# Unread bf16 products on TensorE in five of a quad's eight items of the maximum phase

## What is computed

```python
def _L1_gnn_ref(z, P, W1, b1, W2, b2, Wu, bu):
    m1z = z @ W1.T + b1
    m2z = z @ W2.T + b2
    pair = relu(m1z[:, :, None, :] + m2z[:, None, :, :])
    mask = (swapaxes(P, 1, 2) != 0)[..., None]
    m = max(where(mask, pair, -inf), axis=2)
    return relu(concatenate((z, m), axis=-1) @ Wu.T + bu)
...
h = maximum(layernorm(x), 0)
x = x + _L1_gnn_ref(h, adj, ...)
```

## Times and profile before

| | us |
|---|---|
| median of 3 timed runs | 2086.39 |
| range of them | 2083.98 to 2087.57 |
| the profiled execution | 2077.1 |
| its span, first to last instruction | 2075.3 |
| of it quad 0 of the maximum phase | 26.9 |
| quads 1 to 14 | 414.1 |
| quad 15 | 30.9 |

### The profile page before, as it was taken

The page is one execution under the profiler, slowest core; times in us unless marked ns, Lnnn a source line. Parts: engine busy times, 40 slices in busy tenths (PEclk is TensorE's granted clock), DMA queues, the critical chain, the costliest instruction groups (busy, mean ns, idle before and its releaser), DMA issues. The chain is left out here.

```text
span 2075.3 us, 43855 instructions
## 1 busy us (share of the span) xinstructions
PE 1737.3 (84%) x13771; PEld 1096.7 (53%) x13771; DVE 1727.0 (83%) x2689; ACT 1390.1 (67%) x3229; POOL 597.2 (29%) x449
## 2 busy tenths in 40 slices
PE   2966777777776899897799999999999678988886
PEld 1855556555663666665465555555555234444445
DVE  5878888888875777785799999999999577888887
ACT  0533333333334999895588888888888687888884
POOL 1530000000002544443344444444444211111110
PEclk9989998999887999997999999999999899999999
DMA  6000000000000000000055555555555699999993
GB/s 183 1 13 1 1 0 0 0 0 0 0 1 4 7 6 4 6 6 21 32 224 223 222 222 223 220 223 220 223 220 223 256 371 350 391 376 369 375 342 88
DMA packets 123567, 292.98 MB, mean 141 GB/s; under 512 B 21376, under 2 KB 57608, under 8 KB 123288
## 3 DMA queue, kind: packets, MB, share of 16 engines
q1 hardware_dynamic: 106360, 283.37, 35.9%
q10 hardware_dynamic: 16896, 8.39, 1.4%
q0 software_dynamic: 256, 0.56, 0.1%
HBM read 150.45 MB, written 141.82 MB: 141 GB/s over the span
## 5 line engine op out<-in xcount | busy, mean ns | idle before, releaser
L1316 POOL TENSOR_TENSOR pair_ring<-hd 128x2048 f32 (+1 forms) x64 | 269.5, 4211 | 310.1 <-DVE pair_ring L1341 310.1
L1401 ACT ACTIVATE v_hid<-v_psW 128x1024 f32<-128x1024 f32 x256 | 263.2, 1028 | 84.9 <-PE v_psW L1439 84.9
L771 DVE TENSOR_REDUCE m_part<-m_psS 128x128 f32<-128x2048 f32 (+1 forms) x128 | 258.9, 2023 | 66.1 <-PE m_psS L638 66.1
L1337 DVE TENSOR_TENSOR pair_ring<-v_psX,hd 128x2048 f32<-128x2048 f32 x128 | 292.3, 2289 | 17.1 <-PE v_psW L1439 17.1
L1439 PE MATMUL v_psW<-pair_ring,p_w1T 128*64 128x512 f32 x1024 | 288.5, 596 | 0.0
L1404 ACT ACTIVATE v_junk<-v_psW 128x1024 bf16<-128x1024 f32 x256 | 263.0, 1027 | 0.0
L638 PE MATMUL m_psS<-m_onehot,m_tableT 32*128 32x128 f32 x3584 | 151.8, 307 | 127.7 <-DVE m_part L771 123.4
L1439 PE MATMUL v_psW<-pair_ring,l_w1T 128*64 128x512 f32 (+1 forms) x1024 | 252.5, 587 | 0.0
L1430 PE MATMUL v_psW<-p_ends,v_weights 128*64 128x512 bf16 x1536 | 235.2, 381 | 3.1 <-DMA v_fold<-in_c_fold_dram 3.1
L638 PEld LDWEIGHTS m_psS<-m_onehot,m_tableT 32*128 32x128 f32 x3584 | 128.6, 207 | 147.3 <-issue 78.2
L708 ACT ACTIVATE m_tableT<-m_psTT 128x512 f32<-128x512 f32 (+1 forms) x128 | 69.3, 541 | 202.4 <-PE m_psTT L620 202.1
(11 more groups left out here) (260 smaller groups left out, 3354.9 us busy)
## 6 DMA issues: line engine op xcount, KB each, us to landing
pair_hidden<-v_hid SPq DMA_DIRECT2D x256, 512.0 KB, 2.6
pair_ring<-pair_hidden SPq DMA_DIRECT2D x128, 1024.0 KB, 7.7
adj_ring<-in_adj_dram ACTq DMA_DIRECT2D x16, 256.0 KB, 5.5
x_all<-in_x_dram ACTq DMA_DIRECT2D x16, 256.0 KB, 5.5
out_dram<-x_all SPq DMA_DIRECT2D x16, 256.0 KB, 2.3
pair_scores<-s_rot SPq DMA_DIRECT2D x64, 32.0 KB, 4.6
s_fwd<-pair_scores SPq DMA_DIRECT2D x64, 32.0 KB, 3.9
s_wide<-pair_scores SPq DMA_DIRECT2D x64, 32.0 KB, 5.0
```

The source lines that it names most:

```text
L771: nc.vector.tensor_reduce(part[:, i % 2, r, :], psS[:, :, 0:w].rearrange("z q (c i) -> z i q c", i=N), AX.XY, ALU.max).then_inc(reduced, 1)
L1316: nc.gpsimd.tensor_tensor(D[:, home(u, SLABS - 1), :].rearrange("c (h d i) -> c h d i", h=2, i=N), one, far, ALU.subtract).then_inc(psub_d ...
L1337: nc.vector.tensor_tensor(slab(s), own, windows(hd, n, s)[1], ALU.max).then_inc(max_done, 1)
L1401: nc.scalar.activation(hid[:, s, :], psW[:, buf, :], ACT.Identity, accum_out=hsum[:, bass.ds(m, 1)]).then_inc(evacuated, 1)
```

## The change

`busy` is a new function on TensorE. It waits until the copy of psF that was issued last for the next quad is done (the one of `second` in item 2, the one of `first` in the others), and then runs two bf16 products of 512 columns, the identity with the first 512 columns of the mask, both into psF. Nobody reads them. It is called at the end of items 2, 4, 5, 6 and 7 of every quad but the last.

```diff
@@ -653,6 +653,13 @@
                         last = nc.tensor.matmul(psU[:, b(i)], mT[:, p, b(i)], k.wuT[:, 1, :], start=False, stop=i == G - 1)
                     last.then_inc(u_mm, 1)
 
+                def busy(g, at):
+
+
+                    pe.wait_ge(m2_copied if at == 2 else m1_copied, done(g))
+                    for _ in range(2):
+                        nc.tensor.matmul(psF[:, :], k.identb[:, :], k.mask1[:, 0:QC], start=True, stop=True)
+
                 def quad(g, p, prev, next):
                     for at in range(ITEMS):
                         select(g, *divmod(at, NG))
@@ -670,6 +677,8 @@
                             prepare(g, *divmod(at + 2, NG))
                         elif next:
                             prepare(g + 1, *divmod(at + 2 - ITEMS, NG))
+                        if at in (2, 4, 5, 6, 7) and next:
+                            busy(g + 1, at)
                 turn(0, 0)
                 second(0, 0)
                 first(0, 0)
```

## The result

| | before | changed |
|---|---|---|
| median | 2083.93 us (6 runs) | 2058.93 us (6 runs) |
| range | 2071.26 to 2087.57 | 2046.81 to 2065.35 |
| the profiled execution | 2077.1 | 2046.81 |
| ratio, 95% interval | | 0.9884 (0.9852 to 0.9917) |

Two further comparisons of the same two kernels, on two different chips, gave 0.9875 (0.9829 to 0.9920) and 0.9897 (0.9854 to 0.9940). The change makes the kernel faster by 1.0 to 1.25%, 21 to 26 us by the three ratios; their intervals reach from 0.6 to 1.7%.

A forecast was written before the change was run, and what follows sets the result against it. Bound: rounds between TensorE and VectorE through one buffer psS, partly at half clock. 12.4 + 7.2 us returned, less 6.0 and 2.1 for item 5's pairs, save 11.5 us: from a median of 2086.39 to 2075 us, range 2064 to 2088.

The forecast's parts named there:

- The round of one buffer, and what is paid in it: Maximum phase, single buffer psS: TensorE work inside a reduction's time is free; whatever makes the selection longer or later is paid.
- The price of a pair: Two added products take 0.43 us at full clock or 0.85 at half; in item 5 about 0.4 us, 6.0 us over 15 quads.
- The new waits: Waits for m2_copied in item 2 and m1_copied in the others: taken as zero, at most 0.2 us in item 2.
- The second place of falls (items 6, 7, 0): Clock falls beginning at the end of item 6 or in item 7 vanish, returning 9.0 + 1.6 + 1.8 = 12.4 us.
- The first place (item 5): Falls beginning in item 5 after item 4's pause: half of 14.4 us returned, 7.2 us; 4 to 7 of 14 quads still fall.
- The sum: Maximum phase: 12.4 + 7.2 - 6.0 - 2.1 = 11.5 us saved.
- Together 26.8 us [...] This is the most that the change can return: Half-clock loss of items 5, 7, 6 and 0 over quads 1 to 14, taken as the upper bound on the saving there.
- quad 15 gets no added products: Last quad of the maximum phase: its next is false, so no pairs, and it was expected to stay as before.
- the first (all falls vanish): Quads 1 to 14: every fall vanishes, item 5 pays its pair; 20.8 us saved, 2065.6 us; chance 0.15.
- The second (the first place untouched, the second one gone): Item 5 falls as before, falls around items 6 and 7 vanish; 2.5 us saved, 2084 us; chance 0.18.
- The third (the clock isn't moved): Added products don't move the clock, or only move falls elsewhere; item 5 pays, 9.9 us slower, 2096 us; chance 0.12.
- The fourth (half of the second place returned): About half of the 12.4 us around items 6 and 7 returned, none in item 5; about no change, 2086 us; chance 0.09.

## Why the prediction was wrong

By its own steps:

- **The round of one buffer, and what is paid in it:** right. Pairs in the pauses of items 2, 4, 6 and 7 cost nothing at full clock: item 4 took 3.57 us with and 3.56 without, item 7 3.22 and 3.22.
- **The price of a pair:** right. Item 5 at full clock went from 3.48 to 3.90 us, 0.42 against the 0.4 taken. With a fall it took 5.52 to 5.57, within the 5.1 to 5.9 forecast.
- **The new waits:** free, as taken. Items 2 and 4 kept their length.
- **The second place of falls (items 6, 7, 0):** right. 12.4 us were forecast, and the first pair of profiles has 54.1 - 44.8 = 9.3 in item 7, 49.6 - 48.2 = 1.4 in item 6 and 59.1 - 56.7 = 2.4 in item 0, together 13.1 us.
- **The first place (item 5):** right in number, 6 of 14 slowed where 4 to 7 were forecast. With the price of its own pair the item lost 1.4 us, where the sum had a loss of some 0.5 in quads 1 to 14 (7.2 returned, 5.6 and 2.1 lost). The comparison on which the forecast rested, that a pause of 1.35 us or less had not been followed by a fall, did not hold: all six follow item 4's pause of 1.34 us.
- **The sum:** 11.5 us were forecast for the maximum phase, and quads 0 to 14 of the first two profiles differ by 11.25. So close a match is luck in part: the second place gave 0.7 us more, the first 0.9 less.

Against the base of this comparison, 2083.93 us, the saving was 25.0 us and not 11.4. That is 13.6 of the 16.1 us by which the time was missed; the other 2.5 are the base itself, 2086.39 in the forecast. The steps that failed are two terms of the bound on the saving, both read off one execution.

- **"Together 26.8 us [...] This is the most that the change can return":** this term was read from one execution, as if it were a property of the program. Over four profiles quads 0 to 14 took 441 to 455 us at a full-clock length near 414, so the half clock takes 27 to 41 us of them, 34 on average. The first profile showed the lower end. The changed kernel has been the same in all its profiles, so the missed part, some 7 us, is all saving. Even the rival in which all falls vanish had a saving of only 20.8 us by this bound, less than was measured.
- **"quad 15 gets no added products", hence no saving:** it has no pairs, but its length is not fixed: 26.5 to 29.0 us in the profiles of before, 24.5 to 26.3 in those of the changed kernel, 28.4 and 25.7 on average. These 2.7 us were not in the sum. They rest on few profiles, and no fall in the quads ahead is no cure: with the pauses filled quad 15 took 29.0 us again.

The terms 11.25, 6.7 and 2.7 make the 20.7 us of the traces. The range of 2064 to 2088 allowed for the cases of the change, and nothing for the base or for the bound; single runs of before alone cover 42 us.

Of the rivals, the first (all falls vanish) took place only where more of the pauses was filled. The second (the first place untouched, the second one gone) is nearest to the kernel with pairs in items 6 and 7 alone; it missed that the first place does not stay untouched. The third (the clock isn't moved) is what one-row products do, and what the full ones don't. The fourth (half of the second place returned) did not occur. The rule of the Trainium skill that the third names (TensorE: Matmul & The Clock Gate, "Why this matters for your kernels"), a fall after an idle pause longer than any in quads 0 to 14, doesn't describe these falls: they went away when pauses of 1.2 to 1.8 us were filled, and one-row products, with TensorE busier than before, didn't stop them. That transposes might not count was tried by no run.

What stays open: the intervals of the comparisons, 0.983 to 0.994, hold both the 20.7 us of the traces and the 25 us of the medians, so whether some 4 us more are saved elsewhere isn't settled. Why a given execution of before takes the shorter or the longer pattern isn't settled either.

## What to carry to other kernels

Where TensorE waits for another engine in each round and the granted clock dips, try filling the pauses with products that use the whole array and that nobody reads, as many as the pause holds, into a bank that is free at that moment; put none where there is no pause. Fill all the pauses of the loop: here pairs at one place alone gave nothing that the timed runs could show, and all pauses filled gave 1.4%. And read a loss to the clock from several executions before it is made the bound of a sum, since the pattern of falls differs from one to the next.

## What the runs showed of the hardware

- A product with one row of the array takes about as long as one with 128 (item 5 at full clock 3.82 and 3.90 us with a pair of either) and didn't keep the clock up: with 150 of them in the phase the clock in quads 1 to 14 was 0.85, with as many full ones 0.97.
- The clock fell from 2.4 to 1.2 GHz in quads 0 to 14 of before with no pause above 1.9 us on TensorE (the longest wait in the earlier trace rows; the 1.78 of the prediction is that of quad 8), and with TensorE busy for half of the time in items 4 and 6. In the changed kernel it fell behind a pause of 1.34 us.
- The same program shows different patterns of falls: 77 us at half clock in quads 0 to 14 in two profiles, 125 and 128 in two others. Quads 1 to 14 of the changed kernel's three profiles agree within 0.01 us over 402 us.
- What a stretch at half clock cost depended on whether TensorE had a pause there: item 7, with one, went from 3.22 to 4.07 us when it lay wholly at half clock, and item 5, without one, from 3.48 to 5.07 us at a clock of 0.66.
